# Slot table built ahead of each third chunk, and tokens counted within step 1, in the shared-expert stage of a transformer block

## The reference

```python
logits = t @ gate_w.T                       # 2048 tokens x 16 experts
probs = softmax(logits)
topv, topi = top_k(probs, 6)
topv = topv / sum(topv)                     # weights of the picked experts
...
shared = (silu(t @ sg_w.T) * (t @ su_w.T)) @ sd_w.T
out = x + (routed + shared)
```

## Time and profile before

| | |
|---|---|
| median of 3 runs | 2192.63 us |
| the profiled execution: its own time | 2189.3 us |
| its span in the trace | 2187.3 us |
| PE busy | 97% of the span |
| DVE busy | 53% |
| granted TensorE clock, mean | 0.992 |
| shared-expert stage in the trace | about 1192 to 1420 us |

### The profile page before, as it was taken

How to read it: one execution, slowest core, us unless ns; L and a number is a source line. 1 busy time by engine, 2 the same in 40 slices (tenths; PEclk the granted TensorE clock), 3 DMA queues, 4 the chain that set the end, 5 groups by cost and what they waited for, 6 DMA issues and landing times. The chain is left out here.

```text
span 2187.3 us, 39667 instructions
## 1 busy us (share of the span) xinstructions
PE 2120.0 (97%) x11850; PEld 1849.9 (85%) x11851; DVE 1149.2 (53%) x2520; ACT 721.0 (33%) x1896; POOL 961.4 (44%) x1004
## 2 busy tenths in 40 slices
PE   7899999999999999999998999999999999999996
PEld 6788888988888888988886777689999999999996
DVE  6746556464655646466566776633333333334332
ACT  6634334343433434344345122222222222222221
POOL 3535454544545455364531323434444444444442
PEclk9999999999999999999999999999999999999998
DMA  3214343443434344343435211276767766676443
GB/s 114 89 60 172 120 140 116 157 158 115 152 125 145 115 152 165 115 144 117 146 105 212 87 68 49 76 232 174 227 160 189 199 170 162 162 218 180 82 77 53
DMA packets 140690, 300.62 MB, mean 137 GB/s; under 512 B 16800, under 2 KB 16800, under 8 KB 138592
## 3 DMA queue, kind: packets, MB, share of 16 engines
q1 hardware_dynamic: 115392, 241.26, 31.5%
q0 software_dynamic: 24960, 58.21, 14.1%
q10 hardware_dynamic: 288, 0.53, 0.1%
HBM read 177.51 MB, written 122.42 MB: 137 GB/s over the span
## 5 line engine op out<-in xcount | busy, mean ns | idle before, releaser
L753 POOL TENSOR_TENSOR chunk_hi<-chunk_raw,zero 128x512 fp32r<-128x512 f32 x153 | 159.3, 1041 | 242.4 <-DMA chunk_raw<-in_whole 242.4
L1665 POOL DMA_INDIRECT out<-y,sidx x111 | 177.4, 1598 | 65.5 <-issue 43.9
L979 DVE TENSOR_TENSOR pT_lo<-ps,pT_hi 128x384 fp32r<-128x384 f32 (+2 forms) x256 | 111.1, 455 | 177.1 <-ACT pT_hi L914 172.7
L755 POOL TENSOR_TENSOR chunk_raw<-chunk_raw,chunk_hi 128x512 fp32r<-128x512 f32 x153 | 197.6, 1292 | 12.0
L1812 DVE TENSOR_TENSOR prod<-ps,silu 128x352 f32<-128x352 f32 x111 | 58.2, 524 | 270.2 <-PE ps L69 270.2
L952 DVE SCALAR_TENSOR_TENSOR HS<-ps,rinv,HS 128x512 f32<-128x512 f32 x260 | 176.4, 738 | 1.2 <-PE ps L69 1.2
L1672 POOL TENSOR_TENSOR carry<-ident 128x1 f32<-128x1 f32 x214 | 43.6, 204 | 298.4 <-DVE gidx L1818 198.9
L900 ACT ACTIVATE prob<-ps,negmax 128x512 f32<-128x512 f32 (+3 forms) x256 | 131.7, 527 | 110.1 <-DVE negmax L941 110.1
L1807 DVE TENSOR_SCALAR y<-ps,weight_of 128x512 f32<-128x512 f32 x111 | 83.3, 750 | 133.7 <-PE ps L69 133.1
L67 PE MATMUL ps<-ring,xT_0hi 128*128 x448 | 150.0, 335 | 0.8 <-DMA ring<-split_weights 0.8
L67 PE MATMUL ps<-wv_or_qk_hi,hT_hi 128*128 128x256 f32 x512 | 146.3, 286 | 2.9 <-PEq L134 2.9
(11 more groups left out here) (324 smaller groups left out, 5991.8 us busy)
## 6 DMA issues: line engine op xcount, KB each, us to landing
ring<-split_weights SPq DMA_DIRECT2D x240, 272.0 KB, 6.9
chunk_raw<-in_whole SPq DMA_DIRECT2D x153, 256.0 KB, 2.7
split_weights<-chunk_hi SPq DMA_DIRECT2D x153, 256.0 KB, 2.4
split_weights<-chunk_raw SPq DMA_DIRECT2D x153, 256.0 KB, 2.6
xg<-in_wqk SPq DMA_DIRECT2D x16, 512.0 KB, 3.5
x_spill<-x SPq DMA_DIRECT2D x4, 1024.0 KB, 3.8
xg<-in_wv SPq DMA_DIRECT2D x8, 512.0 KB, 3.4
xg<-in_wo SPq DMA_DIRECT2D x8, 512.0 KB, 4.7
```

The costliest lines, as they stand in the source:

```text
L753: nc.gpsimd.tensor_tensor(chunk_hi[k][:], chunk_raw[k][:], zero[:].to_broadcast([P, CH]), ALU.add).then_inc(chunk_high, 1)
L755: nc.gpsimd.tensor_tensor(chunk_raw[k][:].bitcast(F32R), chunk_raw[k][:], chunk_hi[k][:].bitcast(F32), ALU.subtract).then_inc(chunk_low, 1)
L979: nc.vector.tensor_tensor(pT[1][:, 0:split, w], ps_t[k % 2][:, 0:split * P].rearrange("p (j t) -> p j t", t=P), pT[0][:, 0:split, w].bitca ...
L1665: nc.gpsimd.indirect_dma_start(out, bass.IndirectOffsetOnAxis(ap=sidx[q][:], axis=0), y[q][:], None, bounds_check=T + P - 1, oob_is_err=Tr ...
```

## The change

It has two parts, and neither adds or removes an instruction.

1. Behind the third chunk of a step, DVE makes all three `in_column` tiles before `prod`, where one came after `prod` and two after the low part. ACT runs its lane before the copy of the high part.
2. The two matmuls that count tokens run on PE behind chunk (1, 1), where they stood behind `down(0)`. `count_tokens` runs on DVE behind chunk (1, 2), ahead of the four additions of step 1, where it stood behind them. `place_blocks` follows `place` behind (2, 0), `pack(0)` is behind (2, 1), and nothing is behind (2, 2).

```diff
@@ PE
                     into_table(n, c)
+                    if (n, c) == (1, 1):
+                        pe.wait_ge(dve_r, PICKED)
+                        pe.wait_ge(pool_0, 7)
+                        chosen = sel16[:].rearrange("p t e -> p (t e)")
+                        nc.tensor.matmul(ps_r[:, 0:TT * E], before[:], chosen, start=True, stop=True)
+                        nc.tensor.matmul(ps_c[:, 0:TT * E], ones[:], chosen, start=True, stop=True).then_inc(pe_r, 1)
                 if n >= 1:
                     down(n - 1)
...
-                if n == 1:
-                    pe.wait_ge(dve_r, PICKED)
...
@@ ACT
+                    if c == NI - 1:
+                        last_lane(n, c)
                     act.wait_ge(dve_p, q + 1)
                     w = REST if rest(n, c) else P
                     nc.scalar.copy(hh[n % 2][0][0:w, c, :], prod[0:w, :]).then_inc(act_h, 1)
-                    last_lane(n, c)
+                    if c < NI - 1:
+                        last_lane(n, c)
@@ DVE
+                    if c == NI - 1:
+                        columns(n, c)
                     dve.wait_ge(act_s, q + 1)
                     dve.wait_ge(pe_u, q + 1)
...
-                    columns(n, c, range(ahead(n, c)))
+                    if c < NI - 1:
+                        columns(n, c, range(ahead(n, c)))
...
+                    elif (n, c) == (1, 2):
+                        total = count_tokens()
                     elif (n, c) == (2, 0):
                         ends = place(total)
+                        place_blocks(ends)
                     elif (n, c) == (2, 1):
-                        place_blocks(ends)
-                    elif (n, c) == (2, 2):
                         pack(0)
...
-                    columns(n, c, range(ahead(n, c), RING))
+                    if c < NI - 1:
+                        columns(n, c, range(ahead(n, c), RING))
...
-                if n == 1:
-                    total = count_tokens()
```

## The result

| | median | runs |
|---|---|---|
| kernel before | 2192.01 us | 20 |
| changed kernel | 2196.98 us (2192.62 to 2201.04) | 20 |

The ratio is 1.0025, with an interval of 1.0018 to 1.0032: 5.5 us slower, between 3.9 and 7.0. The forecast was 2196.0, with a range of 2191.3 to 2199.0. The profiled execution of the changed kernel took 2200.83 us, with a span of 2199.0 and a mean granted clock of 0.986, against 2187.3 and 0.992. So 11.7 us lie between the two spans, and the question is how many of them belong to the change.

What follows compares the result with a forecast made beforehand. PE, busy for 97% of the span, was taken as the bound, so only its waits or clock matter. Terms +1.95 - 0.45 + 1.86 = +3.4 us on 2192.6 gave 2196.0 us, range 2191.3 to 2199.0 for 8 in 10.

Steps and rivals of the forecast that it cites:

- The wait for `prod`: Step 1, PE ahead of chunk (1, 1): the 4.0 us wait ends on DVE's step 0 work and stays.
- Term 1: Step 1: counting ahead of the first addition makes PE's third tile of `down(0)` wait; +1.95 us.
- Rival D: Step 1: counting is hidden, PE's third tile of `down(0)` does not wait; +1.4 us, 2194.0 us; chance 0.10.
- Term 2: Step 2: sooner packing covers a DVE wait for PE, shortening PE's wait at the third tile of `down(1)`; -0.45 us.
- Term 3: Third chunks, steps 3 to 7: 1.14 us saved at slot (n, 3) is given back by (n, 4); +1.86 us together.
- Rivals A: Slot (n, 3): columns still meet POOL's lanes and take 1.91 us; +4.6 us, 2197.2 us; chance 0.17.
- C: Third chunks: the stall goes and is not given back; -3.8 us, 2188.8 us; chance 0.12.
- The clock stays at 1.00 behind each new stall: TensorE clock behind the new stalls in step 1 and at slots (n, 4): no fall, no cost.
- Rival B: TensorE clock falls behind six long stalls, about 1.4 us each; +8.4 on +3.4, 2204 us; chance 0.04.

Runs made afterwards that it cites:

- Packing alone: Kernel before with only place_blocks and pack(0) one chunk sooner, counting left behind the additions of step 1; 2189.96 us, ratio 0.9997.
- the second comparison: The changed kernel, unaltered, timed again against the kernel before, beside its two parts on the same chip; 2196.9 us, ratio 1.0021.
- the run with the table before the additions: Columns first behind third chunks, low part put off, and columns ahead of the addition in tile slots of steps 3 to 7; 2186.1 us, ratio 0.9969.

## Why the prediction was right

The terms of the sum came nearly as they were worked out, each by the mechanism that the prediction gave. One step failed, the clock's.

- *The wait for `prod`, 4.0 us, stays.* It did. Its size moved by itself, 3.9 to 5.0 us.
- *Term 1, +1.95.* The third tile of `down(0)` came 2.05 us later on PE's way from chunk (1, 1), of which 0.22 is the moved pair (0.24 predicted) and 1.83 the stall. The stall was 1.67 us, in the predicted 1.6 to 1.9. The 1.83 is this idle time and 0.16 by which a modelled end laps over the next start; with 0.11 for the slow first matmul the term is 1.94. Rival D, counting hidden, is out.
- *Term 2, -0.45.* Packing alone shortened the stall of step 2 by 0.44. In the changed kernel it went from 1.70 to 1.16, by 0.54, just below the 1.3 to 1.7 that the prediction had named as its sign. The -0.63 of the table is this 0.54 and the pair's 0.22, which has left the stretch, less about 0.11 for the slow first matmul, which has come into it. Terms 1 and 2 together: +1.42, predicted +1.50.
- *Term 3, +1.86.* Step 3 gave +0.53 (0.62), steps 4 to 7 +0.30 each (0.31): +1.73. The mechanism was right in each of its parts: the stall at (n, 3) goes, low part and addition stand in front of the next columns, and these run at 1.67 us. Slot (4, 4) came at E + 7.13 with both in front, at E + 6.50 with the low part put off, and at E + 5.82 with the addition behind the columns as well, which shows that they were the cause. Rivals A (columns at 1.91) and C (not given back) are out. The stall at slot (n, 4) was 1.36 to 1.50 us and not "about 1.7": the prediction's own distances, 7.15 - 2.85 = 4.30 where a slot takes 2.85, give 1.45.
- *The clock stays at 1.00 behind each new stall.* This step failed. The profile of the first execution bears it out, and four others don't: 7 falls behind 25 stalls. Rival B had the price right, "about 1.4" us, and was wrong that every stall long enough brings one. The prediction took one row as its evidence, the 1.00 behind a stall of 1.70 us in step 2, and carried it over to stalls at another place. By the tally a run of the changed kernel has 5 x 7/25 = 1.4 falls, 1.4 us each, about 2.0 us. This is an estimate from few executions. With it the sum is 3.15 + 2.0, some 5.1 us, within the measured 3.9 to 7.0 and the 2.4 to 6.8 of the second comparison; without it, 3.15 lies just under the first.

Each execution has its mean clock on record, profiled or not, and these bear the falls out. Over all executions here, before ran at a mean clock of 0.9898 in 2192.1 us (82 of them) and the changed kernel at 0.9886 in 2197.1 us (33). Within either kernel an execution took about 1.35 us longer for each 0.001 that its clock was lower. By this estimate 1.6 us of the difference between the means, 4.9, go with the lower clock, and 3.3 (2.9 to 3.7) are left at equal clock, where the traces give 3.15. The executions of one chip alone, 44 and 13, leave 3.7 (3.1 to 4.3). So the changed kernel does run at a lower clock, which the prediction had at nothing. That it is the falls behind the five stalls is supported and not proved, since a mean clock doesn't show where it fell. The rule cited in the prediction from TensorE: Matmul & The Clock Gate, in the Trainium skill (section "What's actually happening"), that activity releases the throttle, isn't at odds with these rows, but it did not tell which stall brings a fall. Why only steps 5 to 7 have them is open. What stands around the stall differs there, since `down` of steps 4 to 6 has shorter tiles, 8 matmuls of which the last has 64 rows; no run changed that alone.

The measured median, 2196.98, is near 2196.0 although the predicted difference, 3.4 us, was some 2 us short by the ratio: the longer comparison has before at 2192.01, 0.6 below the value that the forecast started from, and its difference of medians is 5.0. That the median came within 1.0 us of the forecast is in that part luck; the traced sum, 3.15 against 3.36, is not.

## What to carry to other kernels

When a stall is removed by moving work ahead, walk the same engine's row to its next deadline: here 1.14 us were saved at one slot and 1.4 lost at the next. Order an engine's work by who waits for it; what nobody waits for soon (the low part, counting) goes behind what PE needs, in pieces no longer than the slack. Replacing stalls of 1.2 us by stalls of 1.5 one slot later cost more than the 0.3 between them, because the clock sometimes fell behind the new ones, and one profile does not show how often.

## What the runs showed of the hardware

- The clock's falls vary from one execution to the next with the same code. One at 1160 to 1168, ahead of anything that differs, moved the start of the stage by 5 us between two executions of the kernel before (1192.16 and 1197.09). Positions in two traces are compared only by distances from a common matmul.
- What POOL's two lanes and DVE's three columns cost each other depends on what DVE is at when the lanes start. With the columns starting within 0.06 us of them: columns 1.82 to 1.91, lanes 1.25 to 1.68. With DVE in its addition, and the columns right behind it: columns 1.66, lanes 2.74, one lane 2.16. SBUF — State Buffer, in the Trainium skill (section "SBUF: two separate sides"), says that where a DVE instruction with two SBUF inputs meets a GpSimd instruction that reads SBUF, whichever starts first holds the shared ports for its whole instruction and the other one is blocked. The columns have two such inputs, and the addition, which reads `ps` and `HS`, has one. The trace agrees in part. The lane of 2.16 us ended at 1318.58, behind the last of the columns at 1318.20, as if blocked by all three. But by the rows it had started first, at 1316.42 against 1316.54, and the order of such starts doesn't tell who waits.
- Reordering kept this away: in the run with the table before the additions, a slot of the table behind a third chunk took 2.83 to 2.96 us, with the same instructions.
